# Startup loads, a split weight split, and the transposes of the last two tiles in a gated cross-attention kernel

## The chip, the cores and the metric

The kernel runs on one core of one Trainium2 chip. Its time is the device time of one execution in microseconds (us). Before the change the median of 3 executions is 1130.98 us (1130.7 to 1131.45).

## The reference

The reference is one Flamingo-style block with 32 batches. The queries come from x (112 rows of 256 features per batch), the keys and values from a context (375 rows of 256 per batch), with 16 heads of 64.

```python
x = x + tanh(g_xattn) * xattn(ctx, layernorm(x), fside, fside, ...)
x = x + tanh(g_ffn)   * ffn(layernorm(x), w1, b1, w2, b2)
# xattn: k, v = layernorm(ctx; ln1) @ Wkv;  q = layernorm(x; ln2) @ Wq
#        q = q * (1 + fside) + fside, by head;  softmax(q k^T / 8) v @ Wout
# ffn:   per row: rmsnorm, rounding to 8 bits, ternary weights; gelu between the two products
```

## The kernel before, in words

**Arithmetic.** Products of the attention are made from pairs of 16-bit numbers, a high and a low part: each product is three matmuls (lines 831 to 836). So every operand is split once: the high part is a rounding, the low part is what is left. The feed-forward part works on integers and ternary weights and needs one matmul.

**Work by batch (0 to 31).** The context rows and query rows of a batch are loaded into one buffer each (lines 342 to 350), each load waiting until the batch before has been normalised. The statistics are VectorE steps BA, BB and BS (lines 763 to 774), the scale is GpSimd step LNA (line 470), the normalisation is ScalarE step LNW (line 590). TensorE then turns the rows: Z0 and Z1 are the two halves of the context, ZX the queries (lines 903 to 911). ScalarE moves them out of the accumulators (ZF0, ZF1, ZXF), GpSimd splits them (ZS0, ZS1, ZXS, lines 457 to 468). K0 to K7 are the key products of 128 columns each (line 879), V00 to V12 the value products, Q0 and Q1 the query products; ScalarE makes the high parts (KH, VH), VectorE the low parts (KL, VL, line 671). S0 to S7 are the scores of a pair of heads; M, E, PH and PL are maximum, exponential, high part and low part of the probabilities (PL on GpSimd, line 444). T0 to T7 are DMA transposes of the probabilities (line 363), A0 to A7 the products with the values (line 855), N0 to N3 the normalisation of four heads (line 676), OO0 and OO1 the turning of the result (line 912).

**Work by tile.** Every 128 rows of the output make one tile (28 tiles, NT). WO is the output projection. X1, XST and SC1 make the residual, its statistics and scales; XR and XQ round it. XD is a DMA transpose of the rounded rows and XTE the clipping on VectorE; F0 and F1 are the first feed-forward product; HE0 and HE1 scale it, GE is gelu, SQ the squares, HMX the maximum, SC2 the scales; HR and HQ round; HD is the DMA transpose, HTE the clipping, F2 the second product, YE the result, ST its store. For tile 27 alone the two transposes are TensorE steps instead, XT and HT (lines 928 to 935), and the clipping reads the accumulators (lines 788 to 795). GpSimd steps RM1 and RM2 (lines 491 and 502) make the two root-mean-square factors, and XB (line 497) adds the bias.

**What sets the order.** Nothing is scheduled at run time. Each engine follows a list written out by hand: FIRST for the start, then ORDER once per batch with offsets, then LAST (lines 49 to 192, put together by `sequence`, line 198). For steps of tiles the lists name batches; a program line turns batch b into tile b - b // 8 - 1, so 31, 30, 29 and 28 in the lists are tiles 27, 26, 25 and 24. The products share three accumulator banks in rotation (line 221): a step waits until the bank's user three places ahead of it in TensorE's list has been moved out. An engine that waits holds everything behind it in its list.

**The weights.** At the start SP issues the loads of the first context and queries, the key weights, the query weights and the value weights (lines 330 to 340). The later ones (output weights, both feed-forward weights, their biases, the gates) go out in `load_late_weights`, called from the load of the queries of batch 1, and so ahead of the load of the context of batch 1. ScalarE splits off the high parts of whole weights (WKH, WQH, WVH, WOH, line 518), VectorE the low parts (WKL, WQL, WVL, WOL, line 645). AS0, AS1, SUM, WM, RW0, RW1, TN0 and TN1 make the ternary weights.

The starts of the lists that the change touches:

```python
FIRST["DVE"] = [
    ("BA", 0), ("BB", 0), ("BS", 0), ("WKL", 0), ("WQL", 0), ("BA", 1), ("KL1", 0), ("BB", 1),
    ("BS", 1), ("KL2", 0), ("KL0", 0), ("WVL", 0), ("KL3", 0), ("KL4", 0), ("AS0", 0), ("M0", 0),
    ("KL7", 0), ("M1", 0), ("KL5", 0), ("BA", 2), ("M2", 0), ("BB", 2), ("KL6", 0), ("M3", 0),
LAST["PE"] = [
...
    ("A1", 31), ("A2", 31), ("A3", 31), ("A4", 31), ("A5", 31), ("F2", 28), ("A6", 31), ("A7", 31),
    ("OO0", 31), ("OO1", 31), ("F0", 30), ("F1", 30), ("WO", 31), ("F2", 29), ("XT", 31), ("F0", 31),
    ("F1", 31), ("F2", 30), ("HT", 31), ("F2", 31),
```

## Time and profile before

| what | value |
| --- | --- |
| median of 3 executions | 1130.98 us (1130.7 to 1131.45) |
| the profiled execution | 1132.53 us |
| its span (first to last instruction) | 1130.7 us |
| mean granted TensorE clock | 0.981 |
| busy: TensorE, ScalarE, VectorE, GpSimd | 1067.6, 970.6, 945.4, 776.6 us |
| mean DMA rate | 114 GB/s |

Times of the trace are microseconds from the start of the span. PE is TensorE, PEld its weight loads, DVE VectorE, ACT ScalarE, POOL GpSimd, and SP the engine that issues the DMAs. In a timeline the bracket at the end of a row tells how long the engine had been idle and what ended that. The granted clock is 1.00 at TensorE's upper level (2.4 GHz) and 0.50 at its lower one (1.2 GHz). A line number L833 is the helper's, so one line stands for the products of many steps. The profiled execution is 1.55 us above the median.

### The profile page before, as it was taken

The page shows a single profiled execution, that of the slowest core. Times are in us where ns is not written, and L with a number is a line of the kernel's source. Part 1 is how long each engine was busy: PE and PEld are TensorE (multiplying, and loading weights), DVE is VectorE, ACT ScalarE, POOL GpSimd, SP SyncE. Part 2 cuts the span into 40 slices and gives each one's busy share as a digit, 9 for nine tenths or more (in the row PEclk, how much of TensorE's full clock was granted, in tenths as well). Part 3 has the DMA queues.
Part 4 walks back from the last instruction along what each step waited for, and adds up shares of the span by engine and source line. Part 5 has one row for each costly group of instructions (what it writes and reads, how often), then busy time and mean ns, then how long its engine had stood idle before and what let it go on. Part 6 is the DMA issues. An engine that isn't in the chain of part 4 may idle for free.

```text
span 1130.7 us, 32113 instructions
## 1 busy us (share of the span) xinstructions
PE 1067.6 (94%) x11900; PEld 733.8 (65%) x11900; DVE 945.4 (84%) x2108; ACT 970.6 (86%) x1864; POOL 776.6 (69%) x839
## 2 busy tenths in 40 slices
PE   2789999999999999999999999999999999999983
PEld 1456666676676676767667666766776676667662
DVE  2688789888889888888988878898888888888984
ACT  4588789999999979999999979999999978999862
POOL 4376667766777777676787766678767767877732
PEclk9799999999999999999999999999999999999986
DMA  8246665676776666679666676756666775765741
GB/s 274 52 95 109 105 103 100 121 117 118 114 138 103 107 117 113 120 110 139 113 101 127 118 116 100 133 112 100 128 109 119 118 136 99 102 127 101 120 107 38
DMA packets 409498, 129.42 MB, mean 114 GB/s; under 512 B 391136, under 2 KB 404192, under 8 KB 409344
## 3 DMA queue, kind: packets, MB, share of 16 engines
q1 hardware_dynamic: 409344, 127.36, 64.2%
q8 instruction: 98, 1.61, 0.6%
q14 instruction: 56, 0.46, 0.1%
HBM read 26.71 MB, written 3.67 MB: 27 GB/s over the span
## 4 chain that ended last, share of the span: by engine, by line
PE 73%; ACT 8%; issue 5%; DMA 4%; DVE 4%; POOL 3%; POOLq 1%; DVEq 1%; SPq 0%; ACTq 0%
PE work L833 15%; PE work L834 15%; PE work L835 15%; PE ps_s L852 10%; DMA pt<-pn 4%; PE ps_o L833 3%; PE ps_o L835 3%; PE ps_o L834 3%; ACT prob L606 2%; PE work L916 2%; PE work L945 2%; ACT q_f L572 2%; PE work L907 2%; PE work L954 2%; ACT L606 2%
## 5 line engine op out<-in xcount | busy, mean ns | idle before, releaser
L447 POOL TENSOR_TENSOR pn<-prob,pn 112x750 f16<-112x750 f32 x256 | 399.3, 1565 | 115.7 <-ACT pn L616 104.6
L606 ACT ACTIVATE prob<-ps_s,neg_max 112x375 f32<-112x375 f32 x512 | 265.2, 573 | 9.0 <-DVE neg_max L748 7.1
L748 DVE TENSOR_REDUCE neg_max<-ps_s 112x2 f32<-112x750 f32 x256 | 237.2, 928 | 24.0 <-PE ps_s L852 24.0
L833 PE MATMUL work<-z,wkv_h 128*128 128x375 f16 x512 | 168.2, 328 | 15.1 <-DVE k_l L673 8.7
L833 PE MATMUL ps_o<-v_h,pt 128*128 128x65 f16 (+1 forms) x1536 | 168.3, 195 | 8.8 <-DMA pt<-pn 5.6
L834 PE MATMUL ps_o<-v_l,pt 128*128 128x65 f16 (+1 forms) x1536 | 168.1, 193 | 0.0
L835 PE MATMUL ps_o<-v_h,pt 128*128 128x65 f16 (+1 forms) x1536 | 168.0, 194 | 0.0
L835 PE MATMUL work<-z,wkv_l 128*128 128x375 f16 x512 | 167.0, 326 | 0.0
L834 PE MATMUL work<-z,wkv_h 128*128 128x375 f16 x512 | 166.9, 326 | 0.0
L529 ACT ACTIVATE k_h<-work 128x375 f16<-128x375 f32 x256 | 121.4, 487 | 50.8 <-PE work L835 45.7
L673 DVE SCALAR_TENSOR_TENSOR k_l<-work,k_h 128x375 f16<-128x375 f32 x256 | 136.0, 540 | 33.6 <-ACT k_h L529 33.5
L833 PEld LDWEIGHTS ps_o<-v_h,pt 128*128 128x128 f16 (+1 forms) x1536 | 144.2, 98 | 23.0 <-DMA pt<-pn 9.6
L833 PE MATMUL work<-wkv_h,z 128*128 128x512 f16 (+1 forms) x384 | 146.8, 382 | 3.3 <-DVE v_l L673 2.3
L834 PEld LDWEIGHTS ps_o<-v_l,pt 128*128 128x128 f16 (+1 forms) x1536 | 143.5, 99 | 9.3
L835 PE MATMUL work<-wkv_h,z 128*128 128x512 f16 (+1 forms) x384 | 145.5, 379 | 0.0
L834 PE MATMUL work<-wkv_l,z 128*128 128x512 f16 (+1 forms) x384 | 145.4, 379 | 0.0
L835 PEld LDWEIGHTS ps_o<-v_h,pt 128*128 128x128 f16 (+1 forms) x1536 | 143.4, 97 | 0.0
L673 DVE SCALAR_TENSOR_TENSOR v_l<-work,v_h 128x512 f16<-128x512 f32 (+1 forms) x192 | 128.3, 681 | 7.5 <-ACT v_h L529 6.7
L529 ACT ACTIVATE v_h<-work 128x512 f16<-128x512 f32 (+1 forms) x192 | 115.6, 603 | 13.1 <-PE work L835 11.3
L616 ACT ACTIVATE pn<-prob 112x750 f16<-112x750 f32 x128 | 107.8, 842 | 0.1
L572 ACT ACTIVATE q_f<-work,side_add,side_mul 128x112 f32<-128x112 f32 x256 | 93.7, 466 | 3.7 <-PE work L835 3.7
L852 PE MATMUL ps_s<-k_h,q_h 64*112 64x375 f16 x512 | 88.7, 343 | 0.7 <-ACT prob L606 0.6
(133 smaller groups left out, 2725.1 us busy)
## 6 DMA issues: line engine op xcount, KB each, us to landing
ctx_in<-in_ctx SPq DMA_DIRECT2D x32, 375.0 KB
pt<-pn SPq DMA_TRANSPOSE x256, 3.4
x_in<-in_x SPq DMA_DIRECT2D x32, 112.0 KB, 3.8
x_res<-in_x SPq DMA_DIRECT2D x28, 128.0 KB, 5.2
out<-y SPq DMA_DIRECT2D x28, 128.0 KB, 2.0
stage<-in_wkv SPq DMA_DIRECT2D x2, 1024.0 KB, 9.3
stage<-in_w SPq DMA_DIRECT2D x2, 1024.0 KB, 10.5
stage<-in_wq SPq DMA_DIRECT2D x1, 1024.0 KB, 8.5
```

Of the source, the lines that this page charges most:

```text
L447: g.tensor_tensor(buf[:, 1, :, 0:SK], prob[:, p % 2], buf[:, 0, :, 0:SK], ALU.subtract).then_inc(p_lo, 1)
L529: a.activation(dst, src, ACT.Identity, scale=1.0 / W_SCALE).then_inc(hi_done, 1)
L572: i = a.activation(q_f[:, c, :], work[:, BANK[job], m * SQ:(m + 1) * SQ], ACT.Identity, bias=add, scale=mul)
L606: i = a.activation(prob[:, p % 2, h, :], ps_s[0:SQ, 2 * (p % 2) + h, 0:SK], ACT.Exp, bias=neg_max[:, 2 * (p % 2) + h:2 * (p % 2) + h + 1])
L616: a.activation(pn[g % PBUF][:, 0, :, 0:SK], prob[:, p % 2], ACT.Identity).then_inc(p_hi_act, 1)
L673: v.scalar_tensor_tensor(out=dst, in0=src, scalar=1.0 / W_SCALE, in1=hi_part, op0=ALU.mult, op1=ALU.subtract).then_inc(evacuated[BANK[job] ...
L748: v.tensor_reduce(neg_max[:, 2 * (p % 2):2 * (p % 2) + 2], ps_s[0:SQ, 2 * (p % 2):2 * (p % 2) + 2, 0:SK], X, ALU.max, negate=True).then_in ...
L833: t_.matmul(dst, sh, mh, start=(n == 0), stop=False)
L834: t_.matmul(dst, sh, ml, start=False, stop=False)
L835: i = t_.matmul(dst, sl, mh, start=False, stop=(n == len(pairs) - 1))
L852: i = t_.matmul(ps_s[0:SQ, 2 * (p % 2) + h, 0:SK], q[r, p, :], k[r, p, :], start=(n == 0), stop=(n == 2))
L907: i = t_.transpose(w[:, t * TP:(t + 1) * TP], ctx_n[:, t, c * P:(c + 1) * P], ident[0:TP, 0:TP])
```

## The change

The late weights become a step of SP's list, LW, and stand behind both loads of batch 1. The splits of the key weights are made in two halves of 512 columns (WKH0, WKH1, WKL0, WKL1), and K0 to K3 wait for the first half only. The split of Z1 of batch 0 (ZS1) moves from GpSimd to VectorE. With TAIL = 2 tiles 26 and 27 are turned by XT and HT on TensorE, and tile 26 needs no XD and HD any more. The lists FIRST and LAST of all five engines are new (their parts that matter are below, only with the new text); ORDER is the same in every engine.

```diff
--- before.py
+++ after.py
@@ -30,6 +30,7 @@
 WORK_BANKS = 3
 NT = B * SQ // P
 RING = 7 * P
+TAIL = 2
 CAST_ACT = (0, 2, 4, 6)
 
 
...
 FIRST["PE"] = [
+    ("Z1", 0), ("Z0", 0), ("K1", 0), ("K0", 0), ("K2", 0), ("ZX", 0), ("K4", 0), ("K3", 0),
+    ("Q0", 0), ("Z0", 1), ("K7", 0), ("K5", 0), ("K6", 0), ("Z1", 1), ("S0", 0), ("S1", 0),
+    ("V02", 0), ("V00", 0), ("K0", 1), ("Q1", 0), ("S2", 0), ("V10", 0), ("V01", 0), ("S3", 0),
+    ("ZX", 1), ("K1", 1), ("S4", 0), ("V11", 0), ("A0", 0), ("A1", 0), ("K3", 1), ("S5", 0),
+    ("S6", 0), ("K2", 1), ("V12", 0), ("K4", 1), ("A2", 0), ("A3", 0), ("Z0", 2), ("S7", 0),
+    ("Q0", 1), ("K7", 1), ("K5", 1), ("A4", 0), ("SUM", 0), ("Z1", 2), ("K6", 1), ("S0", 1),
...
 LAST["PE"] = [
...
+    ("V01", 31), ("V02", 31), ("A6", 30), ("A7", 30), ("OO0", 30), ("S5", 31), ("S6", 31), ("OO1", 30),
+    ("A0", 31), ("V10", 31), ("A1", 31), ("V11", 31), ("F0", 29), ("S7", 31), ("V12", 31), ("F1", 29),
+    ("A2", 31), ("A3", 31), ("WO", 30), ("F2", 28), ("A4", 31), ("A5", 31), ("A6", 31), ("A7", 31),
+    ("XT", 30), ("OO0", 31), ("OO1", 31), ("F0", 30), ("F1", 30), ("WO", 31), ("F2", 29), ("XT", 31),
+    ("F1", 31), ("F0", 31), ("HT", 30), ("F2", 30), ("HT", 31), ("F2", 31),
 FIRST["ACT"] = [
+    ("LNW", 0), ("WKH0", 0), ("ZF1", 0), ("ZF0", 0), ("WQH", 0), ("WKH1", 0), ("KH1", 0), ("WVH", 0),
+    ("KH0", 0), ("KH2", 0), ("ZXF", 0), ("WOH", 0), ("KH4", 0), ("KH3", 0), ("LNW", 1), ("QF0", 0),
+    ("ZF0", 1), ("KH7", 0), ("KH5", 0), ("ZF1", 1), ("KH6", 0), ("VH02", 0), ("E0", 0), ("VH00", 0),
+    ("PH0", 0), ("KH0", 1), ("E1", 0), ("QF1", 0), ("VH10", 0), ("E2", 0), ("TNH", 0), ("VH01", 0),
+    ("PH2", 0), ("E3", 0), ("KH1", 1), ("ZXF", 1), ("VH11", 0), ("E4", 0), ("PH4", 0), ("KH3", 1),
...
 LAST["ACT"] = [
...
+    ("E2", 31), ("KH7", 31), ("PH2", 31), ("XR", 29), ("VH00", 31), ("KH6", 31), ("E3", 31), ("E4", 31),
+    ("VH01", 31), ("VH02", 31), ("HR", 28), ("OH0", 30), ("PH4", 31), ("OH1", 30), ("E5", 31), ("VH10", 31),
+    ("VH11", 31), ("E6", 31), ("PH6", 31), ("E7", 31), ("VH12", 31), ("GE", 29), ("SQ", 29), ("XR", 30),
 FIRST["DVE"] = [
+    ("BA", 0), ("BB", 0), ("BS", 0), ("WKL0", 0), ("ZS1", 0), ("WQL", 0), ("WKL1", 0), ("KL1", 0),
+    ("BA", 1), ("KL0", 0), ("BB", 1), ("KL2", 0), ("BS", 1), ("WVL", 0), ("KL4", 0), ("KL3", 0),
+    ("WOL", 0), ("KL7", 0), ("KL5", 0), ("AS0", 0), ("KL6", 0), ("M0", 0), ("BA", 2), ("VL02", 0),
+    ("M1", 0), ("VL00", 0), ("KL0", 1), ("BB", 2), ("PH1", 0), ("M2", 0), ("VL10", 0), ("M3", 0),
+    ("VL01", 0), ("BS", 2), ("M4", 0), ("KL1", 1), ("PH3", 0), ("VL11", 0), ("AS1", 0), ("M5", 0),
...
 LAST["DVE"] = [
...
+    ("KL7", 31), ("M4", 31), ("KL6", 31), ("VL00", 31), ("N2", 30), ("SC2", 28), ("PH3", 31), ("VL01", 31),
+    ("VL02", 31), ("N3", 30), ("M5", 31), ("M6", 31), ("OT0", 30), ("XTE", 29), ("OT1", 30), ("PH5", 31),
+    ("N0", 31), ("VL10", 31), ("VL11", 31), ("M7", 31), ("HE0", 29), ("HE1", 29), ("VL12", 31), ("PH7", 31),
+    ("N1", 31), ("HTE", 28), ("X1", 30), ("XST", 30), ("YE", 28), ("N2", 31), ("SC1", 30), ("HMX", 29),
+    ("N3", 31), ("XTE", 30), ("SC2", 29), ("OT0", 31), ("OT1", 31), ("HE1", 30), ("HE0", 30), ("X1", 31),
+    ("XST", 31), ("HTE", 29), ("SC1", 31), ("HMX", 30), ("YE", 29), ("XTE", 31), ("SC2", 30), ("HE1", 31),
+    ("HE0", 31), ("HTE", 30), ("YE", 30), ("HMX", 31), ("SC2", 31), ("HTE", 31), ("YE", 31),
 FIRST["POOL"] = [
+    ("LNA", 0), ("ZS0", 0), ("ZXS", 0), ("LNA", 1), ("SD", 0), ("QS0", 0), ("ZS1", 1), ("ZS0", 1),
+    ("PL0", 0), ("PL1", 0), ("QS1", 0), ("PL2", 0), ("LNA", 2), ("PL3", 0), ("PL4", 0), ("GT", 0),
+    ("ZXS", 1), ("PL5", 0), ("QS0", 1), ("ZS0", 2), ("PL6", 0), ("ZS1", 2), ("PL7", 0), ("PL0", 1),
...
 FIRST["SP"] = [
+    ("LX", 1), ("LD", 1), ("LW", 0), ("LD", 2), ("LX", 2), ("T0", 0), ("T1", 0), ("T2", 0),
+    ("T3", 0), ("LD", 3), ("T4", 0), ("LX", 3), ("T5", 0), ("T6", 0), ("T7", 0), ("RS", 1),
...
@@ -348,8 +349,6 @@
                 if b > 0:
                     sp.wait_ge(ctx_normed, b)
                     sp.dma_start(x_in[:], x[b]).then_inc(x_loaded, 16)
-                if b == 1:
-                    load_late_weights()
 
             def load_late_weights():
                 sp.dma_start(gates[:, 0:1], g_x.partition_broadcast(P)).then_inc(small_in, 16)
@@ -392,14 +391,16 @@
             for name, b in sequence("SP"):
                 if name[0] == "T":
                     turn(b, int(name[1]))
-                if name == "XD" and b < NT - 1:
+                if name == "XD" and b < NT - TAIL:
                     turn_quantised(b)
-                if name == "HD" and b < NT - 1:
+                if name == "HD" and b < NT - TAIL:
                     turn_hidden(b)
                 if name == "LD":
                     load_context(b)
                 if name == "LX":
                     load_queries(b)
+                if name == "LW":
+                    load_late_weights()
                 if name == "RS":
                     load_residual(b)
                 if name == "ST":
@@ -484,7 +485,7 @@
                     split_q(b, int(name[2]))
                 if name == "ZXS":
                     split_zx(b)
-                if name in ("ZS0", "ZS1"):
+                if name == "ZS0" or name == "ZS1" and b > 0:
                     split_z(b, int(name[2]))
                 if name == "LNA":
                     layernorm_scales(b)
@@ -530,8 +531,9 @@
 
             def step(name, b):
                 job = (name[0] + name[2:], b)
-                if name == "WKH":
-                    split_hi(0, wk_in, wkv_f[:, :, 0:INNER], wkv_h[:, :, 0:INNER])
+                if name in ("WKH0", "WKH1"):
+                    c = slice(int(name[3]) * HALF, (int(name[3]) + 1) * HALF)
+                    split_hi(0, wk_in, wkv_f[:, :, c], wkv_h[:, :, c])
                 if name == "WQH":
                     split_hi(1, wq_in, wq_f, wq_h[:])
                 if name == "WVH":
@@ -642,12 +644,18 @@
         def _(dve):
             v = nc.vector
 
-            def split_lo(n, w, hi_part, lo_part):
-                dve.wait_ge(hi_split[n], 1)
+            def split_lo(n, w, hi_part, lo_part, count=1):
+                dve.wait_ge(hi_split[n], count)
                 for k in range(w.shape[1]):
                     i = v.scalar_tensor_tensor(out=lo_part[:, k, :], in0=w[:, k, :], scalar=W_SCALE, in1=hi_part[:, k, :],
                                                op0=ALU.mult, op1=ALU.subtract)
                 i.then_inc(lo_split[n], 1)
+
+            def split_z_first():
+                dve.wait_ge(evacuated[BANK["Z1", 0]], USE["Z1", 0])
+                v.tensor_copy(z[0][:, 0, 1], zf[:, 1])
+                dve.drain()
+                v.tensor_tensor(z[0][:, 1, 1], zf[:, 1], z[0][:, 0, 1], ALU.subtract).then_inc(z_ready, 1)
 
             def sum_weight(n):
                 dve.wait_ge((w1_in, w2_in)[n], 16)
@@ -719,8 +727,11 @@
 
             def step(name, b):
                 job = (name[0] + name[2:], b)
-                if name == "WKL":
-                    split_lo(0, wkv_f[:, :, 0:INNER], wkv_h[:, :, 0:INNER], wkv_l[:, :, 0:INNER])
+                if name in ("WKL0", "WKL1"):
+                    c = slice(int(name[3]) * HALF, (int(name[3]) + 1) * HALF)
+                    split_lo(0, wkv_f[:, :, c], wkv_h[:, :, c], wkv_l[:, :, c], int(name[3]) + 1)
+                if name == "ZS1":
+                    split_z_first()
                 if name == "WQL":
                     split_lo(1, wq_f, wq_h, wq_l)
                 if name == "WVL":
@@ -785,18 +796,18 @@
                     x1_statistics(b)
                 if name == "SC1":
                     scales(x1_rms, b, amax1, x1_c, clip1, inv1, qs1, deq1, 0)
-                if name == "XTE" and b == NT - 1:
+                if name == "XTE" and b >= NT - TAIL:
                     dve.wait_ge(full[BANK["XT", b]], USE["XT", b])
                     v.tensor_scalar(xqt[:].rearrange("p c q -> p (c q)"), work[:, BANK["XT", b], :].bitcast(F16)[:, 0:KC * P],
                                     -QMAX - 1, QMAX, ALU.max, ALU.min).then_inc(evacuated[BANK["XT", b]], 1)
-                if name == "HTE" and b == NT - 1:
+                if name == "HTE" and b >= NT - TAIL:
                     dve.wait_ge(full[BANK["HT", b]], USE["HT", b])
                     v.tensor_scalar(hqt[:].rearrange("p c q -> p (c q)"), work[:, BANK["HT", b], :].bitcast(F16)[:, 0:FF // P * P],
                                     -QMAX - 1, QMAX, ALU.max, ALU.min).then_inc(evacuated[BANK["HT", b]], 1)
-                if name == "XTE" and b < NT - 1:
+                if name == "XTE" and b < NT - TAIL:
                     dve.wait_ge(x_turned, 16 * (b + 1))
                     v.tensor_scalar(xqt[:], xqt_r[:], -QMAX - 1, QMAX, ALU.max, ALU.min).then_inc(x_clipped, 1)
-                if name == "HTE" and b < NT - 1:
+                if name == "HTE" and b < NT - TAIL:
                     dve.wait_ge(h_turned, 16 * (b + 1))
                     if b > 0:
                         dve.wait_ge(full[BANK["F2", b - 1]], USE["F2", b - 1])
@@ -879,7 +890,7 @@
                 if name[0] == "K":
                     pe.wait_ge(z_ready, 2 * b + 2)
                     if b == 0:
-                        pe.wait_ge(lo_split[0], 1)
+                        pe.wait_ge(lo_split[0], 1 + int(name[1]) // 4)
                     c = slice(int(name[1]) * P, (int(name[1]) + 1) * P)
                     i = three(w[:, 0:SK], [(wkv_h[:, k, c], wkv_l[:, k, c], zb[:, 0, k, :], zb[:, 1, k, :]) for k in range(KC)])
                 if name[0] == "V":
@@ -936,7 +947,7 @@
                 if name in ("F0", "F1"):
                     if b == 0:
                         pe.wait_ge(tern_ready[0], 1)
-                    if b == NT - 1:
+                    if b >= NT - TAIL:
                         results(b, ["XT"])
                     else:
                         pe.wait_ge(x_clipped, b + 1)
@@ -946,7 +957,7 @@
                 if name == "F2":
                     if b == 0:
                         pe.wait_ge(tern_ready[1], 1)
-                    if b == NT - 1:
+                    if b >= NT - TAIL:
                         results(b, ["HT"])
                     else:
                         pe.wait_ge(h_clipped, b + 1)
```

## Rows read from the trace of the kernel before

**Rows 1.** Stretches: length, busy us (count) by engine, granted clock, DMA share, GB/s.
```profile
20.00:40.00 20.00, 10.16 (x54) 5.38 (x54) 7.29 (x17) 5.45 (x10) 6.16 (x7) 0.74 0.45 166
...
40.00:160.00 120.00, 112.48 (x1203) 73.64 (x1204) 99.68 (x193) 98.43 (x202) 79.74 (x80) 0.99 0.53 95
...
160.00:1000.00 840.00, 834.15 (x9453) 579.24 (x9452) 730.76 (x1660) 764.77 (x1477) 605.51 (x641) 1.00 0.69 116
```

**Rows 2.** Timeline of DVE, 31 to 61 us: start, length, instruction, idle before and releaser.
```profile
31.68 0.75 DVE L766 BATCH_NORM_STATS2 ln_bn<-ctx_in 125x6 f32<-125x256 f32 x2 [10.10 <-DMA ctx_in<-in_ctx]
...
45.82 0.94 DVE L748 TENSOR_REDUCE neg_max<-ps_s 112x2 f32<-112x750 f32 x1 [2.52 <-PE ps_s L852]
...
60.62 2.34 DVE L648 SCALAR_TENSOR_TENSOR wout_l<-stage,wout_h 128x1024 f16<-128x1024 f32 x2
```

**Rows 3.** Timeline of SP's DMA issues, then issue-to-landing, then one stretch of DMA alone.
```profile
13.01 0.34 SPq L350 DMA_DIRECT2D x_in<-in_x  x1
...
14.81 0.43 SPq L358 DMA_DIRECT2D stage<-in_wout  x1
...
21.21 18.80 SPq L345 DMA_DIRECT2D ctx_in<-in_ctx  x2
...
stage<-in_wout SPq DMA_DIRECT2D x1, 1024.0 KB, 7.2
...
29.00:30.00 1.00, 0.00 (x0) 0.00 (x0) 0.00 (x0) 0.00 (x0) 0.00 (x0) 0.50 0.33 129
```

**Rows 4.** Timeline of ACT, 12 to 40 us.
```profile
12.89 1.89 ACT L520 ACTIVATE wkv_h<-stage 128x2048 f16<-128x2048 f32 x1
...
37.63 1.58 ACT L596 ACTIVATE ctx_n<-ctx_in,ln_nb,ln_rs 125x256 f32<-125x256 f32 x3 [11.87 <-POOL ln_nb L474]
```

**Rows 5.** Timeline of POOL, 16 to 48 us.
```profile
16.54 1.69 POOL L468 TENSOR_TENSOR z<-zf,z 128x375 f16<-128x375 f32 x1
...
46.94 0.90 POOL L468 TENSOR_TENSOR z<-zf,z 128x375 f16<-128x375 f32 x1
```

**Rows 6.** Timeline of PE, 20 to 60 us.
```profile
20.60 0.47 PE L833 MATMUL work<-z,wkv_h 128*128 128x375 f16 x1 [5.62 <-POOL z L468]
...
32.94 0.49 PE L833 MATMUL work<-z,wkv_h 128*128 128x375 f16 x1 [7.70 <-DVE k_l L673]
...
40.71 0.70 PE L907 MATMUL work<-ident,ctx_n 125*128 125x125 f32 x3 [2.24 <-DVE k_l L673]
...
60.09 0.32 PE L852 MATMUL ps_s<-k_h,q_l 64*112 64x375 f16 x2
```

**Rows 7.** The chain that ended last, inside one key product: start, length, piece.
```profile
44.22 0.30 PE work L834
44.52 0.16 PE work L835
```

**Rows 8.** Who made DVE wait from 1045 to 1100 us: us, times, longest.
```profile
DVE row_inv L680 <- PE ps_o L835: 2.7, 3, 1.3
```

**Rows 9.** A stretch at the end of the last attention, columns as in rows 1.
```profile
1090.00:1100.00 10.00, 7.58 (x120) 6.76 (x120) 6.72 (x18) 3.83 (x6) 2.02 (x5) 0.66 0.41 90
```

**Rows 10.** Timeline of DVE, then of PE and POOL, 1099 to 1131 us.
```profile
1117.62 0.43 DVE L803 TENSOR_SCALAR stage<-hqt_r 128x1024 f16<-128x1024 f16 x1 [3.72 <-DMA hqt_r<-stage]
1117.96 1.21 DVE L813 TENSOR_REDUCE amax<-stage 128x1 f32<-128x1024 f32 x1
...
1120.77 0.21 DVE L710 TENSOR_SCALAR clip<-amax,g_rs 128x1 f32<-128x1 f32 x1
...
1125.29 0.69 DVE L794 TENSOR_SCALAR stage<-work 128x1024 f16<-128x1024 f16 x1 [3.60 <-PE work L935]
...
1118.19 1.86 PE L954 MATMUL work<-w_t,stage 128*128 128x256 f16 x8 [5.08 <-DVE stage L803]
1124.24 1.01 PE L935 MATMUL work<-ident_h,stage 128*128 128x128 f16 x8 [4.18 <-POOL stage L509]
...
1113.46 1.04 POOL L509 TENSOR_SCALAR stage<-stage 128x1024 f16<-128x1024 f32 x1 [3.22 <-ACT stage L635]
```

More of the change, by code:

```diff
@@ L92 @@
 FIRST["ACT"] = [
-    ("LNW", 0), ("WKH", 0), ("ZF1", 0), ("ZF0", 0), ("ZXF", 0), ("WQH", 0), ("KH1", 0), ("WVH", 0),
[11 rows of a table removed]
[12 rows of a table added]
 ]
 LAST["ACT"] = [
[9 rows of a table removed]
[9 rows of a table added]
     ("OH0", 31), ("OH1", 31), ("HR", 29), ("GE", 30), ("SQ", 30), ("XR", 31), ("HR", 30), ("GE", 31),
```

141 rows, old and new, of the table CAST_ACT are left out of this document.

## The prediction

> **What bounds the kernel now.** I read the page's first part (its busy times stand in the table above), then a cut of the span into stretches, then the timelines of each engine at both ends. In the long middle, which runs the unchanged lists, TensorE is busy for 834.15 of 840 us [rows 1]: the loop is bound by TensorE, and a loop entered earlier by some microseconds ends earlier by as many. What can be had lies at the ends. From 20 to 40 us TensorE works for only 10.16 us of 20, at a mean clock of 0.74; from 40 to 160 us it is idle for another 7.5 us of 120 [rows 1].
>
> The start, read by who waits. VectorE sits idle for 10.10 us until 31.68 for the context of batch 1 [rows 2], and its list has the low halves of K1, K2 and K0 behind that, although TensorE made those products long before; so TensorE, whose banks stay full, waits for 7.70 us at 32.94 [rows 6]. Normalising batch 1 starts at 37.63, after 11.87 us of ScalarE idle [rows 4]. The cause is SP's list: queries at 13.01, then the late weights, and the context at 21.21 [rows 3], behind three 1 MB weights. Before that, TensorE waits 5.62 us until 20.60 for GpSimd to split Z1 and Z0 one after the other [rows 6].
>
> **The change, part by part: the start.** I walk the new lists step by step. A key product is six matmuls, 0.30 us each at the lower clock and 0.16 at the upper [rows 7]: 1.9 and 0.95 us. By their columns a value product is 1.3 us, an A step (36 matmuls of 65 columns) about 1.1, a pair of scores 0.65, at the upper clock.
>
> Key weights in halves: 1.89 us on ScalarE for the whole [rows 4] becomes about 1.0 us ahead of the Z's and 1.0 us behind WQH. The Z's then leave the accumulators at about 14.6 and 15.2. VectorE has the first low half at 15.3 and splits Z1 by 16.2: a cast and a subtraction of 375 columns, which no row of VectorE shows; I take 0.9 us, GpSimd's undisturbed subtraction of that size [rows 5] being the nearest row, with bounds 0.5 and 1.7. GpSimd splits only Z0: 15.2 to about 17.5. So K1 starts at 17.5 rather than 20.60 [rows 6], 3.1 us earlier.
>
> While VectorE splits the query weights, two operands read from the same memory, GpSimd's subtraction takes 1.69 us against 0.90 alone [rows 5]: slowed, and I have let the two Z halves overlap in part. The Trainium skill (SBUF — State Buffer, section "Who interferes with whom") goes further: a VectorE instruction with two inputs in SBUF and a GpSimd instruction that reads SBUF exclude each other, the second blocking until the first is through. By that rule ZS0 would end some 0.7 us later, and the sum below would be about 0.5 us less.
>
> The loads: the context of batch 1 is issued at about 13.4 instead of 21.21. From 29 to 30 us it was the only thing moving, at 0.33 of the DMA engines and 129 GB/s [rows 3], so its 375 KB take some 3 us; behind the value weights it lands between 18 and 20.5. VectorE asks for it after WQL (2.5 us), WKL1 (1.3 us) and KL1, at 21.6. The wait of 10.10 us is gone. What is late next: KH0 and KH2 on ScalarE, then WVL (2.34 us, the size of the row at 60.62 [rows 2]). BS of batch 1 ends at 25.0, and as 5.95 us passed from its first statistics to LNW before (31.68 to 37.63), with 0.4 us for the KL steps between, LNW starts at 28.0: 9.6 us earlier.
>
> The late weights pay for that. The output weights were issued at 14.81 and took 7.2 us [rows 3]; now they go out 0.5 us later and share a third of the engines with a load of 3 us: they land between 22.7 and 25.6, I take 24. WOH, which now stands ahead of KH4, KH3 and LNW on ScalarE, could run at 23.6, so it waits 0.4 us there; nothing on the path feels that up to 26.1, from where its 1.9 us push LNW past 28. The weights behind it are asked for after 35, and issuing LW holds nothing back: SP's next wait, the context of batch 2, is free at 30.1.
>
> LNW ends at 30.1, and Z0 of batch 1 follows at once, where Z1 ran at 40.71 [rows 6]; then K7, K5, K6 and Z1, the first 3.5 us at the lower clock as now, so S0 starts at 35.6. VectorE works through KL7, KL5, AS0 (as many columns as WVL, 2.3 us) and KL6 and reaches M0 at 38.3, against 45.82 [rows 2]. That is 7.5 us, with KL7, KL5, KL6 (1.4 us) and the low half of the output weights (2.34 us, at 60.62 [rows 2]) already done, which before came after M0. On TensorE the walk goes on over two value products, K0, Q1, S2, V10, V01, S3, ZX, K1, S4 and V11 to A0 and A1, done at 51.8. Before, S5 ended at about 60.4 [rows 6]; the new list has 1.6 us more of products done by its mark and 0.65 us of S5 still open: 60.4 - 51.8 + 1.6 - 0.65 = 9.55. Of the 7.5 us of idle left from 40 to 160 us [rows 1] I take half a microsecond off, as the value products are spread more evenly. **Start: 10 us**, bounds 6 (a new stall of the size of those left) and 14 (most of them gone too).
>
> **The end.** First the order up to N3 of batch 31. From 1090 to 1100 TensorE is idle for 2.4 us and runs the other 7.58 at a mean clock of 0.66 [rows 9], worth 5.0 us at the upper one: 5 us could go. The new list puts V10, V11, F0, S7, V12 and F1 between A0 and A2, and WO with F2 between A3 and A4, so that N0 and N1 are covered. Against it: XST of tile 26 stands ahead of N2, which costs TensorE some 1.3 us at A6. And VectorE, whose steps up to N3 are the same set, waits only 2.7 us for the A steps [rows 8] and in smaller groups 2.2 us more from 1045 to 1100: no order brings N3 forward by more than 4.9. I take 2.5, bounds -1.5 and 4.5.
>
> Then tile 26 on TensorE. Its XT replaces a transpose that nothing waits for; 0. For HT: HQ ran from 1113.46 to 1114.5, and HTE had to wait until 1117.62 [rows 10]. Now eight transposes (1.01), HTE from the accumulators (0.69) and F2 (1.86 [rows 10]) end at 1118.4 instead of 1120.05. But the new list has YE, then HMX of tile 27 (1.21 [rows 10]), then SC2: 1118.4 + 0.55 + 1.2 = 1120.15, where SC2 started at 1120.77 [rows 10]. **0.6 us**, bounds 0 and 1.6. After SC2 the chain is unchanged.
>
> **The sum.** 10 + 2.5 + 0.6 = 13.1 us off the profiled execution, 1132.5 to 1119.4; it stands 1.55 us above the median of the runs, so against that 1130.98 - 13.1 = 1117.9, said as 1118.
>
> **The rivals.**
>
> *The new lists bring their own waits.* WOH meets weights that land at 27 or later, or the first softmax steps of batch 0 wait on GpSimd. For it: every engine is held by some single wait in the first 60 us of this trace. Against: the walk found slack in each. The start gives 6 and the end nothing: 1125.
>
> *More than the walk.* The idle of 40 to 160 us also halves, and TensorE keeps its clock to N3: 14 + 4 + 0.6, so 1112.5. For it: in my walk normalising batch 2 no longer waits for GpSimd. Against: nothing was walked beyond S5.
>
> *The gain is swallowed.* Context loads or DMA transposes pace the loop, so that entering it earlier only makes it wait: 1131. The 834.15 of 840 us [rows 1] speak against it; a loop paced from elsewhere would show idle on TensorE.
>
> *Slower: the loop doesn't settle.* The lists of the middle are entered in another relative state, and 7.5 of 120 us [rows 1] is how much idle an unsettled phase has. If the loop kept half of that share, 3% of 840 us instead of 5.85 us, it would cost 25 - 6 = 19 us, against 13 gained: 1137. It decides from 1.6% of extra idle on, about 0.5 us per batch. Against: the same lists settled before, from a rougher start.
>
> **How the numbers follow.** The walk's outcome 0.68 (1113.5 to 1121.5), own waits 0.15, more than the walk 0.10, swallowed 0.03, slower 0.04. A measurement of this kernel can tell about 0.2% (2.3 us) from no change. Faster: 0.68 + 0.15 + 0.10 = 0.93, same 0.03, slower 0.04. To hold the time 8 times in 10 the range takes the walk's whole outcome and reaches to the centres of its two neighbours, 1112.5 and 1125.
>
> **What would show each step.** Right: SP issues two loads at 13.0 and 13.4; no VectorE idle above 2 us between 17 and 35; the first key product at 17.5, LNW of batch 1 near 28, M0 near 38; TensorE as busy in the middle as now; the clock at the upper level up to N3; HTE of tile 26 within 2 us of HQ. Wrong: ScalarE idle ahead of WOH, M0 after 41, or TensorE idle of over 10 us in the middle. The end's term is wrong if the time from the last turn of the loop to N3 stays as it was.

## The result and the profile after

The changed kernel takes 1120.84 us (median of 4 executions, 1120.5 to 1121.15) against 1130.84 us (1130.45 to 1131.45) for the kernel before on the same chip: a ratio of 0.991, 95% interval 0.9895 to 0.9925. It is faster by 10.0 us, as forecast in sign, and 2.8 us above the 1118 that was forecast, inside the range. The profiled execution took 1121.15 us, with a span of 1119.3 us at a mean clock of 0.986; against the profiled execution before that is 11.4 us less, of which 1.2 us are the distance of the two profiled executions from their medians (1.55 and 0.3).

The stretches after, columns as in rows 1 (length, then busy us and count of PE, PEld, DVE, ACT and POOL, granted clock, DMA share, GB/s):

```profile
20.00:40.00 20.00, 16.02 (x95) 9.13 (x93) 15.33 (x29) 12.31 (x23) 7.62 (x12) 0.83 0.57 191
40.00:160.00 120.00, 116.46 (x1304) 77.27 (x1302) 101.22 (x204) 102.60 (x209) 80.70 (x81) 1.00 0.63 105
160.00:1000.00 840.00, 833.47 (x9436) 577.95 (x9435) 731.11 (x1662) 763.89 (x1478) 611.15 (x643) 1.00 0.68 115
```

TensorE works 16.02 us instead of 10.16 in the first stretch and is idle for 3.5 us instead of 7.5 in the second [rows 1]; the middle is as busy as it was. The start, on the timelines of SP, ACT, DVE, POOL and PE in turn (start, length, instruction, idle before and releaser):

```profile
13.57 0.33 SPq L346 DMA_DIRECT2D ctx_in<-in_ctx  x1
...
15.29 0.43 SPq L357 DMA_DIRECT2D stage<-in_wout  x1
...
25.64 1.91 ACT L521 ACTIVATE wout_h<-stage 128x2048 f16<-128x2048 f32 x1 [1.66 <-DMA stage<-in_wout]
28.19 1.57 ACT L598 ACTIVATE ctx_n<-ctx_in,ln_nb,ln_rs 125x256 f32<-125x256 f32 x3
...
15.78 0.74 DVE L658 TENSOR_TENSOR z<-zf,z 128x375 f16<-128x375 f32 x1
...
21.54 0.75 DVE L777 BATCH_NORM_STATS2 ln_bn<-ctx_in 125x6 f32<-125x256 f32 x2
...
24.66 2.73 DVE L650 SCALAR_TENSOR_TENSOR wkv_l<-stage,wkv_h 128x1024 f16<-128x1024 f32 x2
...
33.69 0.55 DVE L681 SCALAR_TENSOR_TENSOR k_l<-work,k_h 128x375 f16<-128x375 f32 x1 [2.46 <-ACT k_h L530]
...
38.69 0.93 DVE L759 TENSOR_REDUCE neg_max<-ps_s 112x2 f32<-112x750 f32 x1
...
16.26 1.01 POOL L469 TENSOR_TENSOR z<-zf,z 128x375 f16<-128x375 f32 x1
25.13 2.02 POOL L473 TENSOR_TENSOR ln_rs<-ln_ve,minus_half 125x4 f32<-125x4 f32 x1
...
17.33 0.50 PE L844 MATMUL work<-z,wkv_h 128*128 128x375 f16 x1 [2.54 <-POOL z L469]
...
30.40 0.86 PE L918 MATMUL work<-ident,ctx_n 125*128 125x125 f32 x3 [3.74 <-ACT x_n L599]
```

The first key product runs at 17.33 (forecast 17.5), the statistics of batch 1 at 21.54 with no wait for their context (21.6), its normalisation at 28.19 (28.0), the first maximum at 38.69 (38.3). Two things went otherwise. The output weights landed at 25.6, the late end of the forecast's span, and ScalarE waited 1.66 us for them, not 0.4. VectorE waited 2.46 us for a key at 33.69, where the forecast had no idle above 2 us.

How far each mark lies ahead of the same mark of before, from the same timelines: the normalisation of batch 1 by 9.44 us, YE of tile 0 by 12.17 (185.67 against 197.84), and so on without change to tile 13; then about 11.5 for the rest of the loop, because TensorE waits 0.97 us at 655.17 for a transpose of probabilities; N3 of batch 31 by 11.00 (1088.59 against 1099.59), the last SC2 by 11.74 (1109.03 against 1120.77 [rows 10]), the span by 11.4. So all of the gain, and a little more, is there before the loop. Nothing is gained between the loop and N3. The loop itself, from YE of tile 0 to YE of tile 21, takes 793.47 us before and 794.07 after; in the four traces with the old first lists it takes 793.1 to 793.9, in the ten with the new ones 793.2 to 795.5. So the new start may lose some tenths of a microsecond again in the loop; no run takes that alone.

The same 114 us up to N3, cut in two, first before and then after:

```profile
986.00:1066.00 80.00, 79.48 (x896) 55.38 (x895) 69.87 (x147) 71.66 (x140) 59.23 (x62) 1.00 0.69 117
1066.00:1099.60 33.60, 30.89 (x391) 22.35 (x388) 27.98 (x63) 24.43 (x40) 16.55 (x17) 0.90 0.58 111
```

```profile
974.50:1054.50 80.00, 77.25 (x903) 54.82 (x901) 70.70 (x146) 70.95 (x134) 57.15 (x60) 1.00 0.57 115
1054.50:1088.60 34.10, 30.84 (x384) 21.46 (x383) 28.20 (x64) 25.51 (x45) 19.16 (x21) 0.98 0.59 118
```

The new order does keep the clock in the second piece, 0.98 instead of 0.90. It pays for that in the first: TensorE is busy for 77.25 us instead of 79.48. Two of the waits there, the second one's cause on VectorE, and what ran beside that on GpSimd:

```profile
1034.34 0.39 PE L844 MATMUL work<-wkv_h,z 128*128 128x512 f16 x1 [1.19 <-DVE k_l L681]
1040.61 0.59 PE L956 MATMUL work<-w_t,xqt 128*128 128x512 f16 x2 [1.13 <-DVE xqt L809]
...
1037.78 2.69 DVE L809 TENSOR_SCALAR xqt<-xqt_r 128x256 f16<-128x256 f16 x1
...
1037.31 3.08 POOL L448 TENSOR_TENSOR pn<-prob,pn 112x750 f16<-112x750 f32 x2 [1.77 <-DVE pn L766]
```

### The profile page after: what moved, and what is told of

It reads as the page before. It is cut to its first block, busy times and chain, and to the rows that moved or that the text cites. A ratio compares the mean times of both kernels' runs of the same rounds, so it can differ in the third digit from the quotient of the medians.

```text
span 1119.3 us, 32134 instructions
## 1 busy us (share of the span) xinstructions
PE 1068.0 (95%) x11910; PEld 733.5 (66%) x11910; DVE 946.4 (85%) x2112; ACT 970.7 (87%) x1865; POOL 772.1 (69%) x837
## 4 chain that ended last, share of the span: by engine, by line
PE 78%; ACT 9%; DMA 5%; issue 3%; DVE 2%; POOL 1%; POOLq 0%; DVEq 0%; SPq 0%; ACTq 0%
PE work L844 16%; PE work L846 16%; PE work L845 16%; PE ps_s L863 11%; DMA pt<-pn 4%; PE ps_o L844 3%; PE ps_o L846 3%; PE ps_o L845 3%; PE work L927 3%; ACT prob L608 2%; ACT q_f L574 2%; ACT L608 2%; PE work L956 2%; PE work L918 2%; PE work L965 2%
## 5 line engine op out<-in xcount | busy, mean ns | idle before, releaser
L759 DVE TENSOR_REDUCE neg_max<-ps_s 112x2 f32<-112x750 f32 x256 | 237.6, 929 | 21.6 <-PE ps_s L863 21.5
L844 PE MATMUL ps_o<-v_h,pt 128*128 128x65 f16 (+1 forms) x1536 | 166.5, 194 | 9.1 <-DMA pt<-pn 7.6
L681 DVE SCALAR_TENSOR_TENSOR k_l<-work,k_h 128x375 f16<-128x375 f32 x256 | 136.4, 541 | 38.4 <-ACT k_h L530 38.3
L846 PE MATMUL ps_o<-v_h,pt 128*128 128x65 f16 (+1 forms) x1536 | 166.3, 193 | 0.0
L844 PEld LDWEIGHTS ps_o<-v_h,pt 128*128 128x128 f16 (+1 forms) x1536 | 143.4, 97 | 22.5 <-DMA pt<-pn 10.4
L530 ACT ACTIVATE v_h<-work 128x512 f16<-128x512 f32 (+1 forms) x192 | 115.3, 601 | 11.4 <-PE work L846 9.5
## 6 DMA issues: line engine op xcount, KB each, us to landing
stage<-in_w SPq DMA_DIRECT2D x2, 1024.0 KB, 13.1
```

The costliest lines, as they stand in the source:

```text
L530: a.activation(dst, src, ACT.Identity, scale=1.0 / W_SCALE).then_inc(hi_done, 1)
L681: v.scalar_tensor_tensor(out=dst, in0=src, scalar=1.0 / W_SCALE, in1=hi_part, op0=ALU.mult, op1=ALU.subtract).then_inc(evacuated[BANK[job] ...
L759: v.tensor_reduce(neg_max[:, 2 * (p % 2):2 * (p % 2) + 2], ps_s[0:SQ, 2 * (p % 2):2 * (p % 2) + 2, 0:SK], X, ALU.max, negate=True).then_in ...
L844: t_.matmul(dst, sh, mh, start=(n == 0), stop=False)
L846: i = t_.matmul(dst, sl, mh, start=False, stop=(n == len(pairs) - 1))
```

## The experiments

Twelve kernels were run, in three groups, each timed beside the kernel before (its medians 1130.52, 1130.63 and 1131.12). One execution differs from the next by about 1.4 us (standard deviation of 17 executions of the kernel before, 1129.19 to 1133.02), so medians of 4 to 6 tell differences above some 2 us, and smaller ones are read from the traces. A trace is of one execution, and what it shows need not hold in the others of its kernel. In the expectations S is the theory that the start gave the whole gain and the new end nothing, P the prediction's own division (start 10, order 2.5, tile 26 0.6). To compare ends, marks are given from YE of tile 21 on, the last mark of the loop. In the cuts of the lists, ... stands for what is left out.

**The change again, in the group of the ends.**

> The change once more, on the chip and beside the kernels of this group, so that its end can be compared with the others. Both theories: 10 us faster than before, 1120.5 (1119.5 to 1121.5).

1121.05 us (1120.1 to 1121.85), ratio 0.9915 [0.9903, 0.9927]. YE of tile 0 lies 11.6 us ahead of before, N3 108.20 us behind YE of tile 21, against 108.28 before and 108.85 in the first trace of the change.

**The start alone:** FIRST of all engines, load order, key halves and Z1 on VectorE; LAST and TAIL as before.

```diff
-LAST["PE"] = [ ("Q0", 30), ("K4", 30), ("Z1", 31), ...
+LAST["PE"] = [ ("Q0", 30), ("Q1", 30), ("A2", 29), ...
-TAIL = 2
+TAIL = 1
```

> The new start with the old end (LAST lists and TAIL = 1 of before). Theory S (the start made all of the gain and more, as the two traces read side by side): LNW of batch 3 to 10 about 12.2 us earlier than before, N3 of the last batch 12 earlier, no gain of the second-to-last tile: 1130.8 - 11.8 = 1119.0, range 1118.2 to 1119.9. Theory P (the terms of the prediction, start 10 and end 3.1, scaled to the 10.0 measured: start about 7.6): 1123 to 1124.

1120.72 us (1117.35 to 1121.79), ratio 0.991 [0.9894, 0.9926]: as fast as the whole change.

**The end alone:** LAST and TAIL = 2 on the start of before (the opposite edit).

> The old start with the new end (LAST lists of the change, TAIL = 2). Theory S: N3 of the last batch half a microsecond later than before, 0.7 us back between N3 and the last SC2: 1130.8 + 0.5 - 0.7 = 1130.6, range 1130.0 to 1131.3. Theory P: 3.1 us faster, 1127.7. A third view, that the new end only loses when it is entered from the new start: 1129 or less.

1132.43 us (1131.7 to 1134.43, 11 executions), ratio 1.0018 [1.0008, 1.0027]: nothing gained, a little lost, and 1.1 us slower than the slowest time expected (1131.3). With the run before it, the term of 3.1 us that the prediction gave the end has fallen.

**The load order alone,** on the kernel before:

```diff
-    ("LX", 1), ("LD", 1), ("LD", 2), ("LX", 2), ...
+    ("LX", 1), ("LD", 1), ("LW", 0), ("LD", 2), ("LX", 2), ...
-                if b == 1:
-                    load_late_weights()
+                if name == "LW":
+                    load_late_weights()
```

> The kernel before with one edit: the late weights are issued behind the load of the context of batch 1. If the load order carries most of the start: the VectorE wait of 10.1 us for the context goes; the first K3 product comes at about 25.5 instead of 32.9 and the maximum of batch 0 is 7 to 8 us earlier; 1130.8 - 7.5 = 1123.3 (1121.5 to 1125). If the context still queues behind the value weights or the splits and lists were the cause: under 3 us, 1128 or more.

1120.26 us (1119.38 to 1123.08), ratio 0.9912 [0.9898, 0.9927]. One step of SP's list, moved, gives what the whole change gives, 3 us more than was expected of it. The six executions lie in two groups, four at 1119.4 to 1120.3 and two at 1122.6 and 1123.1, and the trace is of the slowest.

**The load order with a better end,** and the start of before otherwise (no halves, Z1 on GpSimd). The end is the one described further down under SC2 of tile 27.

```diff
-TAIL = 1
+TAIL = 2
+    ("XT", 30), ("OO0", 31), ...
-    ... ("F1", 31), ("F2", 30), ("HT", 31), ("F2", 31),
+    ... ("F1", 31), ("HT", 30), ("F2", 30), ("HT", 31), ("F2", 31),
-    ... ("HMX", 31), ("YE", 30), ("SC2", 31), ("HTE", 31), ("YE", 31),
+    ... ("HMX", 31), ("SC2", 31), ("YE", 30), ("HTE", 31), ("YE", 31),
```

> The kernel before with two things alone: the late weights behind both loads of batch 1, and the old last lists with tile 26 turned on TensorE and SC2 of tile 27 ahead of YE of tile 26 (that end saved 3.5 us from tile 21's YE on in the trace). No split halves, no z half on VectorE, old first lists. If these are worth the 2.2 us by which the traces differ at the entry of the loop, this kernel takes 1117.8, against 1115.6 with them; if they are worth only what the medians of two kernels differed by, 0.7, it takes 1116.3.

1115.65 us (1113.58 to 1117.59), against 1115.62 for the same end with the new start (the kernel under SC2 of tile 27): halves, Z1 on VectorE and the new FIRST lists are worth nothing that these runs can tell from zero. The load order alone and this kernel have the same start, so why do their traces enter the loop 2.4 us apart (YE of tile 0 at 187.76 and at 185.35)? The load order alone, POOL, DVE, ACT, DVE again and a stretch:

```profile
25.51 1.04 POOL L472 TENSOR_TENSOR ln_rs<-ln_ve,minus_half 125x4 f32<-125x4 f32 x1 [2.74 <-DVE ln_ve L694]
26.70 1.13 POOL L474 TENSOR_TENSOR ln_nb<-ln_nm,ln_rs 125x4 f32<-125x4 f32 x1
...
26.55 2.35 DVE L648 SCALAR_TENSOR_TENSOR wkv_l<-stage,wkv_h 128x1024 f16<-128x1024 f32 x2
...
27.86 1.58 ACT L596 ACTIVATE ctx_n<-ctx_in,ln_nb,ln_rs 125x256 f32<-125x256 f32 x3 [1.81 <-POOL ln_nb L474]
...
36.05 0.94 DVE L748 TENSOR_REDUCE neg_max<-ps_s 112x2 f32<-112x750 f32 x1 [2.52 <-PE ps_s L852]
...
30.00:40.00 10.00, 8.05 (x46) 4.71 (x47) 7.15 (x10) 8.72 (x17) 3.99 (x5) 0.83 0.19 63
```

and this kernel, the same:

```profile
26.69 0.20 POOL L476 TENSOR_TENSOR ln_nb<-ln_nm,ln_rs 125x4 f32<-125x4 f32 x1
...
26.75 0.55 DVE L675 SCALAR_TENSOR_TENSOR k_l<-work,k_h 128x375 f16<-128x375 f32 x1 [0.62 <-ACT k_h L531]
27.21 2.55 DVE L650 SCALAR_TENSOR_TENSOR wkv_l<-stage,wkv_h 128x1024 f16<-128x1024 f32 x2
...
26.92 1.59 ACT L598 ACTIVATE ctx_n<-ctx_in,ln_nb,ln_rs 125x256 f32<-125x256 f32 x3 [0.20 <-POOL ln_nb L476]
...
33.81 0.94 DVE L750 TENSOR_REDUCE neg_max<-ps_s 112x2 f32<-112x750 f32 x1 [0.94 <-PE ps_s L854]
...
30.00:40.00 10.00, 8.71 (x59) 4.81 (x60) 9.06 (x15) 9.46 (x19) 5.89 (x7) 1.00 0.23 72
```

GpSimd's tiny operation started 0.01 us apart in the two. Where VectorE had just begun the split of the value weights it took 1.13 us, where VectorE began later, 0.20. That is 0.94 us at the normalisation and 2.2 at the first maximum. The two traces part before that, on TensorE: its key products, alike until 24.2, go over from 0.31 us for a matmul to 0.16 at 24.4 in the load order alone and at 25.7 in this kernel. So it is in this kernel that VectorE waits 0.62 us for the high part of a key, begins the split 0.66 us later and misses GpSimd's operation. The 0.94 us are the collision; the rest of the 2.2 goes with the clock behind it, 0.83 from 30 to 40 us there and 1.00 here. No instruction differs.

**Z1 of batch 0 back on GpSimd,** in the change:

```diff
-                if name == "ZS0" or name == "ZS1" and b > 0:
+                if name in ("ZS0", "ZS1"):
-    ("LNA", 0), ("ZS0", 0), ("ZXS", 0), ...
+    ("LNA", 0), ("ZS1", 0), ("ZS0", 0), ("ZXS", 0), ...
```

> The change with the first half of z split on GpSimd again, ahead of the second, as before. The prediction's walk gave VectorE's part some 0.7 to 1 us of the first key product: by it K1 starts at 18.5 to 20.0 instead of 17.33 and the loop is entered at most 1 us later, 1121 to 1122 us. If what comes after the first keys (the context of batch 1, the ScalarE steps ahead of its normalisation) sets the path, K1 starts later by as much, LNW of batch 1 stays at 28.2, and the time stays at 1121.0.

1123.77 us (1120.12 to 1125.1), ratio 0.9934 [0.9917, 0.9951]: by medians 2 to 3 us more than the change in its own groups, more than expected; the fastest of the six executions is as fast as the change. K1 at 19.40 was right, but what follows was not 1 us late: POOL, DVE and ACT of this kernel:

```profile
27.09 3.08 POOL L473 TENSOR_TENSOR ln_rs<-ln_ve,minus_half 125x4 f32<-125x4 f32 x1 [0.23 <-DVE ln_ve L702]
30.32 2.20 POOL L475 TENSOR_TENSOR ln_nb<-ln_nm,ln_rs 125x4 f32<-125x4 f32 x1
...
26.93 2.34 DVE L650 SCALAR_TENSOR_TENSOR wkv_l<-stage,wkv_h 128x1024 f16<-128x1024 f32 x2
...
30.12 2.34 DVE L650 SCALAR_TENSOR_TENSOR wout_l<-stage,wout_h 128x1024 f16<-128x1024 f32 x2
...
32.55 1.58 ACT L598 ACTIVATE ctx_n<-ctx_in,ln_nb,ln_rs 125x256 f32<-125x256 f32 x3 [4.32 <-POOL ln_nb L475]
```

The first scale operation starts 1.96 us later than in the change, and the two take 5.3 us instead of 2.02 + 0.20, each ending only behind a weight split of VectorE; the normalisation, which had 0.7 us to spare in the change, is 4.36 us late and YE of tile 0 4.74 (190.41). The change doesn't have the second of these collisions: there the second operation is through at 27.5, before the output weights' split begins at 28.88. The first collision alone costs nothing even at full length: in the start alone the first operation takes 3.08 us as well, and the normalisation still starts at 28.26.

**The key weights split whole,** in the change (WKH0 and WKL0 over all 1024 columns):

```diff
-                    c = slice(int(name[3]) * HALF, (int(name[3]) + 1) * HALF)
-                    split_hi(0, wk_in, wkv_f[:, :, c], wkv_h[:, :, c])
+                    split_hi(0, wk_in, wkv_f[:, :, 0:INNER], wkv_h[:, :, 0:INNER])
```

> The change with the key weights split whole, ahead of the Z's, in the new lists. By the walk K1 starts some 2 us later (19.5) and what is behind it is later by 1 to 2 us: 1122 to 1123 us. If the half split is only cover that nothing waits for, LNW of batch 1 stays within 0.5 us of 28.2 and the time at 1121.0.

1123.81 us (1121.0 to 1124.84), ratio 0.9933 [0.9917, 0.9949]. The same picture: K1 at 18.96, the two scale operations 3.08 and 2.20 us, normalisation at 31.79. So in the new lists, as far as one trace of each shows it, both small steps are needed to get GpSimd's operations through ahead of the output weights' split; in the old lists neither is. Here too one execution in six, of 1121.0, is as fast as the change.

**Tile 26 by DMA, in the new lists:** XD and HD of tile 26 back on SP, XT and HT out.

```diff
-TAIL = 2
+TAIL = 1
-    ("XT", 30), ("OO0", 31), ("OO1", 31), ("F0", 30), ...
+    ("OO0", 31), ("OO1", 31), ("F0", 30), ...
```

> The change with tile 26 turned by DMA again (TAIL = 1, XT and HT of tile 26 taken from TensorE's list, XD and HD put back for SP), all else as in the change. If turning on TensorE brings the gain of the last tiles: HTE of tile 26 waits for the DMA, about 3.1 us after HQ instead of 1.9, and since YE and HMX follow one after the other the last SC2 is 1.2 to 1.6 us later: 1.4 us slower than the change. If the new lists were the only thing that mattered: same as the change within 0.4 us.

1125.07 us (1122.32 to 1126.87), ratio 0.9949 [0.9934, 0.9963]: 4.0 us above the change in the same group, where 1.4 were expected. Both products wait, XTE and F0, then HTE and F2:

```profile
1090.34 0.23 DVE L809 TENSOR_SCALAR xqt<-xqt_r 128x256 f16<-128x256 f16 x1 [1.41 <-DMA xqt_r<-xq]
...
1108.51 0.43 DVE L814 TENSOR_SCALAR stage<-hqt_r 128x1024 f16<-128x1024 f16 x1 [3.71 <-DMA hqt_r<-stage]
...
1090.71 0.88 PE L956 MATMUL work<-w_t,xqt 128*128 128x512 f16 x2 [1.06 <-DVE xqt L809]
...
1109.09 1.86 PE L965 MATMUL work<-w_t,stage 128*128 128x256 f16 x8 [5.07 <-DVE stage L814]
```

From N3 to X1 of tile 27 it takes 8.05 us instead of 5.85, to the last SC2 24.26 instead of 20.44. The transposes of tile 26 are worth 2.2 us (XT) and 1.6 us (HT) here.

**Tile 26 on TensorE in the old last lists:** the start alone, and TAIL = 2.

```diff
+    ... ("A7", 31), ("XT", 30), ("OO0", 31), ...
+    ... ("F1", 31), ("HT", 30), ("F2", 30), ("HT", 31), ("F2", 31),
```

> New start, the LAST lists of before, TAIL = 2 with XT and HT of tile 26 put into TensorE's old list. The old VectorE list has HMX of tile 27 ahead of YE of tile 26, the new one behind it. Theory S: against the kernel with the old end (TAIL = 1) SC2 of tile 27 starts when YE of tile 26 is through, that is some 2.1 us after F2 instead of 3.4: 1.9 us faster than that kernel, 1117.1 (1116.3 to 1118), and faster than the change itself. If the transpose by DMA was no bound there: the same as that kernel within 0.4 us.

1118.41 us (1116.46 to 1121.68), ratio 0.9897 [0.988, 0.9913]. Means differ by 1.5 us from the start alone, within their noise; in the traces N3 to the last SC2 takes 19.24 us instead of 20.83 (this trace is of the fastest of the five executions, 1116.46). The old list has HMX of tile 27 ahead of YE of tile 26, where it runs while VectorE would wait for F2. The new list swapped the two, so its 20.44 has HMX's 1.21 us on the path, and 1.2 us is also what lies between the two.

**SC2 of tile 27 ahead of YE of tile 26** as well, with two columns for the scale that YE still reads:

```diff
-v.tensor_scalar(deq2t[:], deq2[:], tanh_f[:], None, ALU.mult)
+v.tensor_scalar(deq2t[:, b % 2:b % 2 + 1], deq2[:], tanh_f[:], None, ALU.mult)
-    ... ("HMX", 31), ("YE", 30), ("SC2", 31), ("HTE", 31), ("YE", 31),
+    ... ("HMX", 31), ("SC2", 31), ("YE", 30), ("HTE", 31), ("YE", 31),
```

> Old end lists with TAIL = 2 as in the fourth kernel, and SC2 of tile 27 ahead of YE of tile 26 (two columns for the scale, so that the later tile doesn't overwrite it). In that kernel's trace SC2 stands behind YE, which waits 2.15 us for F2 of tile 26. If the wait for F2 is what holds the last scales: SC2 starts when HMX ends, 1.4 us earlier; 1.2 us faster than the fourth kernel, 1117.2 (1116.2 to 1118). If RM2 or HMX hold it anyway: no gain.

1115.62 us (1114.48 to 1116.12), ratio 0.9865 [0.9853, 0.9878], 0.6 us below the range expected. It is 5.4 us faster than the change in the same group. N3 to SC2 takes 17.72 us, 1.5 less than in the kernel before it; the medians of the two, from different groups, differ by 2.8, and their scatter covers the distance from 1.5. On VectorE:

```profile
1102.63 1.21 DVE L825 TENSOR_REDUCE amax<-stage 128x1 f32<-128x1024 f32 x1
1103.91 0.21 DVE L719 TENSOR_SCALAR clip<-amax,g_rs 128x1 f32<-128x1 f32 x1
...
1104.86 0.48 DVE L833 SCALAR_TENSOR_TENSOR y<-work,deq2t,stage 128x256 f32<-128x256 f32 x1
```

**N0 of batch 31 early:** A1 right behind A0, and N0 ahead of XST of tile 26.

```diff
-    ("A0", 31), ("V12", 31), ("V10", 31), ("A1", 31), ...
+    ("A0", 31), ("A1", 31), ("V12", 31), ("V10", 31), ...
```

> The kernel before it, with A1 of batch 31 right behind A0 and N0 ahead of XST of tile 26. If TensorE's 1.8 us idle and its fall to the lower clock from 1093 on come from N0 standing behind XST: the stretch from A0 to N3 is 2 to 4 us shorter and the clock stays up: 1114.5 (1113.5 to 1116). If VectorE's total work bounds N3: under 1 us.

1115.49 us (1115.05 to 1116.56), ratio 0.9867 [0.9854, 0.988]: no gain. The waits of 1.82 us at A2 and 0.82 at A4 became one of 1.87 at A4, for N1. N3 stands 106.16 us behind YE of tile 21, inside what the old order shows without this edit (105.55 to 108.28).

**And XST of tile 26 behind N1:**

```diff
-    ("N0", 31), ("XST", 30), ("VL11", 31), ("VL12", 31), ("VL10", 31), ("N1", 31), ...
+    ("N0", 31), ("VL11", 31), ("VL12", 31), ("VL10", 31), ("N1", 31), ("XST", 30), ...
```

> The kernel with the early N0 (1115.5), and XST of tile 26 behind N1 of batch 31 as well. In that kernel TensorE waits 1.87 us at A4 for N1, which stands behind XST (2.2 us of VectorE) and three low halves. If XST is what is late, the wait falls to about 0.8, TensorE keeps its upper clock up to N3, and the time is 1114.0 to 1114.5. If the low halves are (they end when the last value product ends), or if XST only meets the next wait at A6, nothing is gained: 1115.5.

1117.57 us (1116.65 to 1118.76), ratio 0.988 [0.9861, 0.9898]: slower than without. PE:

```profile
1080.63 0.19 PE L845 MATMUL ps_o<-v_h,pt 128*128 128x65 f16 x1 [0.95 <-DVE attn L691]
1084.81 1.87 PE L966 MATMUL work<-w_t,stage 128*128 128x256 f16 x8 [2.92 <-DVE stage L815]
```

The wait at A4 fell to 0.95, and the next one came: F2 of tile 24 waits 2.92 us for its clipping. XST, moved from ahead of N1 to behind it, now runs between N1 and that clipping, and the clipping then waits 1.06 us for its DMA transpose, 0.35 without the edit.

## Why the prediction came out as it did

**The start: right in mechanism and size (forecast 10).** The walk's marks held to within 0.4 us up to the first maximum. At the entry of the loop the gain is 12.2 us in the first trace, 11.6 in the repeat and 12.0 in the start alone; at tile 21 it is 11.6, 10.3 and 10.4, in part because TensorE waits for transposes of probabilities that the trace of before got in time (0.97 us at 655.17 in the first; 1.11 and 0.68 us in the start alone). The start alone gives 9.8 us by its median, 10.4 by its mean. TensorE's idle from 40 to 160 us fell by 4.0 us, where the walk had taken off only half a microsecond: it had stopped at S5. Two of the signs that it had named went against it, ScalarE's idle ahead of WOH and VectorE's 2.46 us, and the first maximum came within 0.4 us of its time all the same. But the start's gain was put down to four things, and one made it. What failed is the share of the others. The walk had K1 earlier by 3.1 us and followed that to the end as if all were needed; under the old lists the load order alone does as well. The new lists put the splits of the value and output weights behind the statistics of batch 1. There, by the traces without the halves and without Z1 on VectorE, they hold up both of GpSimd's scale operations, and these two steps win back what that costs.

The prediction copied the 5.95 us from the first statistics to the normalisation [rows 2, 4] and did not look inside. In the trace of before they hold the same collision:

```profile
34.45 1.04 POOL L472 TENSOR_TENSOR ln_rs<-ln_ve,minus_half 125x4 f32<-125x4 f32 x1 [11.88 <-DVE ln_ve L694]
35.63 1.97 POOL L474 TENSOR_TENSOR ln_nb<-ln_nm,ln_rs 125x4 f32<-125x4 f32 x1
```

with the value weights' split on VectorE at 35.19. At this place the exclusion that the prediction gave an alternative sum for is seen plainly: GpSimd's two operations take as little as 1.04 and 0.20 us free, but 2.02 or 3.08 and 1.13, 1.97 or 2.20 beside a weight split. The Trainium skill's rule (SBUF — State Buffer, section "Who interferes with whom"), that a VectorE instruction with two SBUF inputs and a GpSimd instruction that reads SBUF exclude each other, agrees with these rows. At Z0 of batch 0, where the prediction looked, it cost next to nothing, 1.01 us against 0.90 [rows 5], as VectorE's subtraction was nearly over when GpSimd's began.

**The order up to N3 (forecast 2.5): wrong, it gave nothing.** N3 stands 108.85 and 108.20 us behind YE of tile 21 against 108.28 before. The prediction read only the new list from A0 of batch 31 on, where it saw rightly that N0 and N1 are covered, and took what the stretch of 10 us [rows 9] had to lose. The list is new from batch 30 on, and in its first 80 us it holds 2.2 us more idle, among it 1.19 us for a low half of a key product and 1.13 us for XTE. That term stood in the sum at nothing. The bound from below, -1.5, held; the value taken did not.

Side by side, the traces of the kernels with either set of last lists show both halves of the bargain (the two with N0 moved are left out):

| last lists | traces | TensorE busy in the 75 us from YE of tile 21 | clock in the 10 us up to N3 | N3 behind YE of tile 21 |
| --- | --- | --- | --- | --- |
| old | before, load order, SC2 first | 74.5 to 74.6 us | 0.66 | 108.28, 108.01, 107.93 us |
| old | start alone, load order with a better end | 74.6 us | 0.83 | 106.88, 106.90 us |
| old | tile 26 on TensorE | 74.6 us | 1.00 | 105.55 us |
| new | the change | 72.25 us | 0.93 | 108.85 us |
| new | change again, end alone, Z1 on GpSimd, keys split whole, tile 26 by DMA | 72.2 to 72.3 us | 1.00 | 108.04 to 108.36 us |

So the covering of N0 and N1 works: the new order keeps the clock in five traces of six. It pays 2.3 us of idle for that in every one of the six. And the clock that was to be gained is partly luck. The old order waits 1.82 and 0.82 us at the same places in all six of its traces, and the clock behind them comes out at three levels. The two furthest apart, kernels with the old last lists and TAIL = 2:

```profile
1080.00:1085.00 5.00, 4.12 (x103) 3.84 (x100) 4.23 (x13) 1.64 (x3) 1.14 (x3) 1.00 0.51 107
```

```profile
1080.00:1085.00 5.00, 4.93 (x68) 4.43 (x69) 3.24 (x9) 1.64 (x3) 1.14 (x3) 0.50 0.25 56
```

(the first is the kernel with tile 26 turned, the second the one with SC2 first as well). The prediction took one trace's 0.66 for the kernel's own.

**Tile 26 on TensorE (forecast 0.6): right in sum, wrong in parts.** The last SC2 moved ahead by 0.74 us relative to N3 in the first trace and 0.8 in the repeat. "Its XT replaces a transpose that nothing waits for; 0" held for the old list only. In the new one WO, XST and SC1 of tile 26 stand late enough that the DMA way costs 2.2 us, and HT is worth 1.6. Of that 3.8 us, 1.2 go for HMX behind YE, as the prediction counted, and the rest, it seems (no run takes it alone), for the later place of tile 26.

**The sum.** Forecast 13.1 us off the profiled execution; it came to 11.4: start 12.2, then -0.75 for a late transpose in the loop, -0.45 up to N3, +0.74 to SC2, -0.3 behind it. The medians gained 10.0. Of the 2.8 us by which 1118 missed, 1.7 are what the end and the loop fell short by less the start's surplus, and 1.2 lie in the two profiled executions; why the one of before was slow isn't shown. Three of the rivals didn't take place: WOH met weights at 25.6, just short of the 26.1 from where the walk had it felt, and the loop is as busy as before, so it neither swallowed the gain nor failed to settle. Both conditions of "more than the walk" did come true, half the idle of 40 to 160 us and the clock kept up to N3; its 1112.5 didn't, for the idle in the part of the last lists that nobody had walked. So that the time came out within 2.8 us is in part luck: a start 2.2 us better than forecast stood against an end that gave 2.8 us less than its 3.1.
